# Two PSUM pairs for the expert gate and up products, and a simpler guard on the projection weight ring, in a two-layer transformer kernel

## The reference

```python
    def _L1_attn_ref(x, Wq, bq, Wk, bk, We, Wr, Wc, bc, Wo, bo):
        ...
        q = (x @ Wq + bq).reshape(b, l, h, dk)
        k = (x @ Wk + bk).reshape(b, l, h, dk)
        ...
        qn = _l2norm(q.transpose(0, 2, 1, 3))
        kn = _l2norm(k.transpose(0, 2, 1, 3))
        escore = jnp.einsum('bhnd,bhde->bhne', qn, we)
        rscore = jnp.einsum('bhnd,bhde->bhne', kn, wr)
        score = jnp.concatenate((escore, rscore), axis=-1)
        out = score @ Wc + bc
        out = out.transpose(0, 2, 1, 3).reshape(b, l, h * dk)
        return out @ Wo + bo

    def _L1_ffn_ref(hidden_states, w_router, w_gating, w_gate, w_up, w_down):
        ...
        g = jnp.einsum('bsh,ehf->ebsf', x, w_gate)
        u = jnp.einsum('bsh,ehf->ebsf', x, w_up)
        h = jax.nn.silu(g) * u
        expert_out = jnp.einsum('ebsf,efh->ebsh', h, w_down)
        ...
        out = jnp.einsum('ebsh,bse->bsh', expert_out, cw)
        return out
```

## Time and profile before

| what | us |
|---|---|
| runs of the kernel before | 23274.12 and 23642.73 |
| their median | 23458.42 |
| the profiled execution, its own time | 22038.47 |
| its span, first to last instruction on the slowest core (core 3) | 22036.9 |
| spans of the eight cores | 21971.6 to 22036.9 |

### The profile page before, as it was taken

One profiled execution on the slowest core, in us unless ns is written; L12 is line 12 of the kernel. 1 busy time (PEld: TensorE's weight loads), 2 busy tenths in 40 slices (PEclk: granted clock), 3 DMA queues, 4 the chain that ended last, 5 costly groups with the idle time before them and its releaser, 6 DMA issues.

```text
span 22036.9 us, 138009 instructions; the slowest of 8 cores (21971.6 to 22036.9 us)
## 1 busy us (share of the span) xinstructions
PE 11858.8 (54%) x44866; PEld 4560.7 (21%) x44866; DVE 5109.2 (23%) x7522; ACT 2521.8 (11%) x2906; POOL 146.3 (1%) x248
## 2 busy tenths in 40 slices
PE   0135454545445454554434444577777777777776
PEld 0011111111111111112333221222222223222232
DVE  2452222222222222223333332111111111111111
ACT  0002121211111121220000001100000000000000
POOL 0000000000000000000000000000000000000000
PEclk9855555555555555555555566899999999999999
DMA  8201211212130303003444311244444444444444
GB/s 152 82 26 18 28 22 25 26 20 31 16 36 11 43 4 46 1 1 81 111 107 117 93 33 25 67 101 101 102 104 99 100 101 101 104 100 101 101 104 111
DMA packets 3082943, 1461.89 MB, mean 66 GB/s; under 512 B 2851717, under 2 KB 2853442, under 8 KB 3073634
## 3 DMA queue, kind: packets, MB, share of 16 engines
q1 hardware_dynamic: 3057250, 1211.17, 22.8%
q0 software_dynamic: 25024, 241.90, 8.5%
HBM read 1627.36 MB, written 238.64 MB: 85 GB/s over the span
## 4 chain that ended last, share of the span: by engine, by line
PE 48%; DVE 20%; ACT 11%; DMA 8%; issue 8%; another core or an unknown queue 4%; DVEq 1%; ACTq 0%; POOLq 0%; SPq 0%; POOL 0%
PE psAll L2487 9%; PE psAll L2491 8%; PE psAll L2541 8%; ACT ar_probsT L1175 7%; PE psAll L1155 5%; DVE ar_mtmp L1078 4%; PE psAll L1185 4%; DVE ar_h_moe L2509 3%; PE psAll L1188 3%; ACT ar_silu_sb L2502 3%; PE psAll L1066 2%; DMA ar_w2sb<-w2q_hbm 2%; DMA ar_w1sb<-w1q_hbm 2%; PE psAll L1424 1%
## 5 line engine op out<-in xcount | busy, mean ns | idle before, releaser
L2487 PE MATMUL psAll<-ar_x1n,ar_gsb 128*128 128x512 bf16 x8192 | 2011.2, 390 | 1843.9 <-DVE ar_h_moe L2509 1810.2
L1175 ACT ACTIVATE ar_probsT<-psAll 128x1024 bf16<-128x1024 f32 x1536 | 1574.0, 1025 | 6769.2 <-PE psAll L1155 6769.2
L1185 PE MATMUL psAll<-ar_probsT,ar_V_tm 128*65 128x512 bf16 x1536 | 932.8, 607 | 1952.0 <-ACT ar_probsT L1175 1952.0
L2491 PE MATMUL psAll<-ar_x1n,ar_usb 128*128 128x512 bf16 x8192 | 1971.5, 384 | 0.0
L2509 DVE TENSOR_TENSOR ar_h_moe<-psAll,ar_silu_sb 128x512 bf16<-128x512 f32 x1024 | 708.0, 691 | 4973.7 <-ACT ar_silu_sb L2502 4973.7
L2541 PE MATMUL psAll<-ar_h_moe,ar_dsb 128*128 128x512 bf16 x8192 | 1778.2, 379 | 61.6 <-DVE ar_h_moe L2509 54.5
L1066 PE MATMUL psAll<-ar_K_ext,ar_Q_ext 64*128 64x512 bf16 x2304 | 1338.0, 582 | 467.0 <-DVE ar_mtmp L1078 439.5
L1078 DVE TENSOR_REDUCE ar_mtmp<-psAll 128x1 f32<-128x512 f32 x2304 | 1486.9, 686 | 251.5 <-PE psAll L1066 219.5
L2502 ACT ACTIVATE ar_silu_sb<-psAll 128x512 f32<-128x512 f32 x1024 | 612.2, 598 | 7296.8 <-PE psAll L2491 7296.7
L1155 PE MATMUL psAll<-ar_Q_ext,ar_K_ext 65*128 65x512 bf16 (+1 forms) x2560 | 1296.8, 589 | 240.2 <-DMA ar_attn_h<-ar_odd_sc 96.1
L2487 PEld LDWEIGHTS psAll<-ar_x1n,ar_gsb 128*128 128x128 bf16 x8192 | 742.2, 99 | 3125.8 <-issue 2429.4
(11 more groups left out here) (402 smaller groups left out, 5867.5 us busy)
## 6 DMA issues: line engine op xcount, KB each, us to landing
ar_gsb<-gate_bf SPq DMA_DIRECT2D x1024, 256.0 KB, 3.3
ar_usb<-up_bf SPq DMA_DIRECT2D x1024, 256.0 KB, 4.0
ar_dsb<-down_bf SPq DMA_DIRECT2D x1024, 256.0 KB, 2.7
ar_w1sb<-w1q_hbm SPq DMA_DIRECT2D x544, 256.0 KB, 3.3
ar_w2sb<-w2q_hbm SPq DMA_DIRECT2D x544, 256.0 KB, 3.0
gate_bf<-w_gate POOLq DMA_DIRECT2D x8, 8192.0 KB, 79.7
up_bf<-w_up POOLq DMA_DIRECT2D x8, 8192.0 KB, 155.5
down_bf<-w_down POOLq DMA_DIRECT2D x8, 8192.0 KB, 216.3
```

Of the source, the lines that this page charges most:

```text
L1175: e.activation(probsT[:, kc % 2, :], ps_st[:], AF.Exp).then_inc(sa.h, 1)
L1185: e.matmul(psE[:, 0:512], V_tm[:, kc, :], probsT[:, kc % 2, 0:512], start=(kc == 0), stop=(kc == p2_kc - 1), skip_group_check=True)
L2487: e.matmul(psA, gsb[:, buf, ic, :], x1n[:, ic, tt_], start=(ic == 0), stop=(ic == NCH - 1), skip_group_check=True)
L2491: ins = e.matmul(psB, usb[:, buf, ic, :], x1n[:, ic, tt_], start=(ic == 0), stop=(ic == NCH - 1), skip_group_check=True)
```

## The change

Two edits, in q1 and in q2. The order of instructions on every engine is the same as before, and so is every transfer; what changes is which counts three kinds of instruction wait for, and which PSUM bank and which half of `silu_sb` a step uses.

In q1, the table `wr_ms` is gone. Each load of a projection weight slice now waits for `sm.n`, that is for every matmul group written before it, the step just before it included.

In q2, step `hc` uses `psA` and `psB` when `hc` is even and `psC` and `psD` when it is odd, and `silu_sb` has two halves used in the same way. TensorE's step waits for the silu and the multiply of step `hc - 2` (kept in `slh_ms` and `hh_ms`), and the first two steps of an expert tile wait for what had been emitted when the tile began. The silu no longer has a wait on VectorE for `hc == 0`.

```diff
-                    widx = t * 24 + wi * NCH + oc
-
-                    def f_lq(e, wi=wi, oc=oc, buf=buf, lw=lw,
-                             gm=wr_ms.get(t * 24 + wi * NCH + oc - 3, 0),
-                             cwt=cw_tot):
+
+                    def f_lq(e, wi=wi, oc=oc, buf=buf, lw=lw, gm=sm.n, cwt=cw_tot):
                         if gm:
                             e.wait_ge(sm.h, gm)
                         e.wait_ge(cast_w.h, cwt)
...
                     smq = sm.inc(1)
-                    wr_ms[widx] = smq
...
-                def f_lo(e, oc=oc, buf=buf, lw=lw,
-                         gm=wr_ms.get(t * 24 + 16 + oc - 3, 0)):
-                    if gm:
-                        e.wait_ge(sm.h, gm)
+
+                def f_lo(e, oc=oc, buf=buf, lw=lw, gm=sm.n):
+                    e.wait_ge(sm.h, gm)
...
-        silu_sb = AR.carve("silu_sb", [128, 512], F32)
+        silu_sb = AR.carve("silu_sb", [128, 2, 512], F32)
...
+                g0sa, g0sv = sa.n, sv.n
+                slh_ms, hh_ms = {}, {}
                 for hc in range(HCH):
...
-                    def f_mg(e, ei=ei, tt=tt, tt_=tt_, hc=hc, buf=buf, lg=lg, lu=lu,
-                             gsa=sa.n, gsv=sv.n):
+                    pg = psA if hc % 2 == 0 else psC
+                    pu = psB if hc % 2 == 0 else psD
+                    gsa2 = slh_ms.get(hc - 2, g0sa)
+                    gsv2_ = hh_ms.get(hc - 2, g0sv)
+
+                    def f_mg(e, tt_=tt_, buf=buf, lg=lg, lu=lu,
+                             pg=pg, pu=pu, gsa=gsa2, gsv=gsv2_):
                         e.wait_ge(lg[0].h, lg[1])
                         e.wait_ge(lu[0].h, lu[1])
                         e.wait_ge(sv.h, gsv)
                         e.wait_ge(sa.h, gsa)
                         for ic in range(NCH):
-                            e.matmul(psA, gsb[:, buf, ic, :], x1n[:, ic, tt_],
+                            e.matmul(pg, gsb[:, buf, ic, :], x1n[:, ic, tt_],
...
-                            ins = e.matmul(psB, usb[:, buf, ic, :], x1n[:, ic, tt_],
+                            ins = e.matmul(pu, usb[:, buf, ic, :], x1n[:, ic, tt_],
...
-                        if hc == 0:
-                            e.wait_ge(sv.h, gsv2)
-                        e.activation(silu_sb[:], psA, AF.Silu).then_inc(sa.h, 1)
+                        e.activation(silu_sb[:, hc % 2], pg,
+                                     AF.Silu).then_inc(sa.h, 1)
                     sasl = sa.inc(1)
+                    slh_ms[hc] = sasl
...
-                        e.tensor_tensor(h_moe[:, hc, :], psB, silu_sb[:],
+                        e.tensor_tensor(h_moe[:, hc, :], pu,
+                                        silu_sb[:, hc % 2],
                                         ALU.mult).then_inc(sv.h, 1)
-                    sv.inc(1)
+                    hh_ms[hc] = sv.inc(1)
```

More of the change, by code:

```diff
@@ L2038, in q1 @@
         cw_tot = cast_w.n
-        wr_ms = {}
         for t in range(4):
@@ L2360, in q1 @@
                 buf = (2 * NCH + oc) % 3
-                widx = t * 24 + 16 + oc
-                def f_lo(e, oc=oc, buf=buf, lw=lw,
-                         gm=wr_ms.get(t * 24 + 16 + oc - 3, 0)):
-                    if gm:
-                        e.wait_ge(sm.h, gm)
+                def f_lo(e, oc=oc, buf=buf, lw=lw, gm=sm.n):
+                    e.wait_ge(sm.h, gm)
                     e.dma_start(out=wring[:, buf],
@@ L2385, in q1 @@
                 smo = sm.inc(1)
-                wr_ms[widx] = smo
                 P.emit("tensor", f_mo)
@@ L2496, in q2, with f_sl, f_h @@
                     P.emit("tensor", f_mg)
-                    def f_sl(e, hc=hc, smv=g_ms[(ei, tt, hc)], gsv2=sv.n):
+                    def f_sl(e, hc=hc, smv=g_ms[(ei, tt, hc)], pg=pg):
                         e.wait_ge(sm.h, smv)
-                        if hc == 0:
-                            e.wait_ge(sv.h, gsv2)
-                        e.activation(silu_sb[:], psA, AF.Silu).then_inc(sa.h, 1)
+                        e.activation(silu_sb[:, hc % 2], pg,
+                                     AF.Silu).then_inc(sa.h, 1)
                     sasl = sa.inc(1)
+                    slh_ms[hc] = sasl
                     P.emit("scalar", f_sl)
-                    def f_h(e, hc=hc, sasl=sasl, svcb=svcb):
+                    def f_h(e, hc=hc, sasl=sasl, svcb=svcb, pu=pu):
                         e.wait_ge(sa.h, sasl)
                         e.wait_ge(sv.h, svcb)
-                        e.tensor_tensor(h_moe[:, hc, :], psB, silu_sb[:],
+                        e.tensor_tensor(h_moe[:, hc, :], pu,
+                                        silu_sb[:, hc % 2],
                                         ALU.mult).then_inc(sv.h, 1)
-                    sv.inc(1)
+                    hh_ms[hc] = sv.inc(1)
                     P.emit("vector", f_h)
```

## The result

| | us |
|---|---|
| changed kernel, median of 11 runs | 20467.13 (20401.42 to 21371.92) |
| kernel before, median of 10 runs | 23243.77 (22539.48 to 23642.73) |
| ratio | 0.865, 95% interval 0.8626 to 0.8674 |
| profiled execution of the changed kernel | 20823.85 |

What follows compares the result with a forecast made beforehand. It took TensorE, ScalarE and VectorE working one after the other in the experts' gate/up steps as the bound. 22,037 - 1,944 + 356 gave 20,450 us profiled; 23,458 - 1,588 gave the forecast 21,870 us, range 20,400 to 22,400.

Steps and rivals of the forecast that it cites:

- The second pair, -1,944 us: q2 gate/up steps: a second PSUM pair removes TensorE's wait, 1.96 us in each of 992 steps, saving 1,944 us.
- The loads at nothing: q2 gate and up weight loads: they keep up at 152 GB/s with the shorter step and add no time.
- The rival of the loads: q2 gate and up slices: loads no faster than now take the wait's place, 23,814 us; chance 0.04.
- The guard, +356 us: q1 projection steps: without prefetch, 96 gaps of 3.2 us and matmuls at the lower clock level cost 356 us.
- at a granted clock of 0.5: q1, sign to look for: TensorE's projection matmuls wait 3.2 us for DMA, 96 times, at this granted clock.
- The sum, 20,450 us for an execution like the profiled one: Whole kernel: profiled span 22,037 - 1,944 + 356, plus 1.6 us, gives 20,450 us, 7.2% less.
- Carrying the 1,420 us over: Whole kernel: the earlier timed median's 1,420 us above the profiled execution was kept unchanged, giving 21,870 us.
- The estimate of 1,228 us by the Trainium skill's page: Experts: a peak-current limiter holding the clock at 13/16 would add 1,228 us to 24,576 matmuls.
- The reason given for carrying it, that both terms are gaps and latencies: Both q1 and q2 terms consist of gaps and latencies, not full-clock matmul time, so the 1,420 us stay.
- the denser matmuls are slowed more: Expert gate/up loops: once without gaps they lose up to 27% of 3,547 us, +947, 22,817 us; chance 0.11.
- if the clock in the gate/up loops falls below the 0.99 of today: q2 gate/up loops: a clock under 0.99 in the changed kernel's profile would show the prediction wrong.
- timed like the profiled one: Whole kernel: timed runs lack the extra 1,420 us and come out at 20,450 us; chance 0.12.

Runs made afterwards that it cites:

- e8: The changed kernel run again without further edits, beside the kernel before on another chip: median 20419.5 us, ratio to before 0.9257.
- e4: The changed kernel run again without further edits, beside the kernel before on one chip: 20,362 us on dies at full clock, ratio 0.9271.
- e3: The kernel before with only the simpler q1 guard, one PSUM pair kept: 22,360 us on dies at full clock, ratio 1.0193.
- e5: The changed kernel plus fillers, 8 unread matmuls behind each Q, K and output projection step but a loop's last: median 20301.06 us, ratio 0.9203.

## Why the prediction was right and wrong

- *The second pair, -1,944 us:* right. The clean dies show -1,995; the step is 3.46 us as summed. Missing were the 15 to 27 steps a core of the gapped loop that take more than 7 us because the clock falls in them: the mean step before is 5.47 us, not 5.42, and the few steps of one window couldn't show that.
- *The loads at nothing:* right, 155 GB/s at a share of 0.73. The rival of the loads falls.
- *The guard, +356 us:* right in both pieces: +359, with a gap of 3.33 us (3.2 forecast) and nearly all matmuls at the lower level. The filler experiment confirms the clock's piece. The sign "at a granted clock of 0.5" came true only in part: up to 0.75 is granted, but mostly in the waits.
- *The sum, 20,450 us for an execution like the profiled one:* right. Undisturbed runs take 20,391 to 20,467 us, a ratio of 0.926 (e8) where the sum gives 0.928.
- *Carrying the 1,420 us over, "I carry the difference over as it is":* this step failed. It treated what two runs had in common as a constant of the kernel. It is the price of a state of the die, up to 1,660 us in a run of the kernel before, which many runs of either kernel don't have; six of the 11 by which the changed kernel was timed did not. The estimate of 1,228 us by the Trainium skill's page had named a mechanism of that size, and I didn't let it into the sum. The 0.865 is thus not what the change is worth: side by side it is 0.926. That the measured time still lies in the range is no merit of the forecast's mechanism; the range had been stretched for the rival.
- *The reason given for carrying it, that both terms are gaps and latencies:* right within some 200 us, where both kernels are held throughout. A held tile costs 41 us with gaps and 35 without, so the change would be worth a little more there, not less: the rival "the denser matmuls are slowed more" had the sign reversed. (Its 3,547 us are 16,384 × 0.2165; 1,024 × 3.46 is 3,543.)
- *The sign of being wrong "if the clock in the gate/up loops falls below the 0.99 of today":* the first profile of the changed kernel shows it, at 0.80, and e4's, at 1.00, does not. It was a sign of the die's state and not of the change.
- *The rival "timed like the profiled one", at 0.12:* this is what happened. With two runs of one kernel and a profile 5.6 and 7.3% below them, it deserved more.

What stays open: why none of the first ten runs of the kernel before was clean, what brings the held clock about, and whether the start times of a die's cores have a part in it.

## What to carry to other kernels

Where ScalarE and VectorE finish a step while TensorE waits, a second set of PSUM banks is worth the gap times the steps, and a loop elsewhere in the trace that runs the same shape without gaps gives the new step time. A guard that is one group too strict cost, here, the whole load latency and, on top, the clock of the matmuls beside it; one slice ahead was enough to hide both. When timed runs and profile of the same kernel differ by more than their own spread, find out what the difference is, by die and clock, before adding it to anything, and compare two kernels only side by side.

## What the hardware showed beside that

- A die's clock can be held in part of the experts: matmuls 0.263 us apart instead of 0.2165. In e3 the two dies differed in one execution, 22,363 and 22,648 us in the median.
- A gapped loop on a held die falls, for about 20 of the 31 steps of most tiles, into a regular pattern of 6.17 and 7.48 us.
- One execution of e5 took 25,165 us, 24% more than its other runs, with the clock of its slowest core at half or below nearly all along. The five other runs of the same kernel took 20,276 to 20,309 us. The clock alone doesn't account for it: cores 2 and 3 took 24,363 and 24,470 us at mean clocks of 0.808 and 0.818. The cause is open. The slowest core's clock in 40 slices:

```profile
PEclk8444444444444444444444444444555555555555
```
